# The last layer's value chunk moved from one PSUM bank to another in a four-layer attention and expert kernel

## The chip, the cores and the metric

One core of a Trainium2 chip runs the whole program. The time is device microseconds (us) from one launch, and lower is better. The engines named below are PE (TensorE, matmuls; PEld are its weight loads), DVE (VectorE), ACT (ScalarE), POOL (GpSimd) and SP (SyncE, which issues DMAs). Each engine runs its own list of instructions in the order written; they meet at semaphores only. PE writes into PSUM, which has eight banks of 128 partitions x 512 fp32 values; ACT and DVE read results out of it. A bank may be written again only when the engine that reads it is done, and that is what the waits in this case are about.

## The reference

Input x is 32 batches x 128 rows x 128 columns. Four layers follow each other, each an attention over a fixed context and then a feed-forward part, always as x = x + f(layernorm(x)): layer 0 and layer 3 have a top-2 mixture of 8 experts, layer 1 a quantised gated unit, layer 2 a router over 64 slots with a GRU step. The last layer's attention, which the change touches, is

```
q = x @ Wq                                  # 128 -> 1024 = 16 heads of 64
k, v = split(context @ Wkv)                 # 128 -> 2048
attn = softmax(q k^T / 8) per head
out = concat(attn @ v) @ Wout + bout        # 1024 -> 128
```

## The kernel before

x stays in SBUF. The 32 batches are handled in 8 groups of 4 (512 rows a group). The program has three phases; the third is where layer 1's down projection, layers 2 and 3 and the last experts are interleaved. Its time is cut into half steps `hs`. In each half step every engine has a list of short pieces, called `work(place, hs)`, at three places (0, 1, 2) between the fixed pieces of one attention unit (scores, exps, transposes, values times probabilities). Tables written by hand say which piece goes where.

A unit of layer 2 is 8 heads of one batch. A unit of layer 3 is a chunk of two heads for the 4 batches of a group; 8 chunks make a group. Layer 3's chunks stand at every second half step. For chunk c of group g:

- three half steps ahead, PE forms the query chunk (line 1774, "q" below) at place 0, and the key chunk (line 1781, "k") at place 2 of the same half step;
- two half steps ahead, PE forms the value chunk (lines 1807, "V" below, 8 records since each fp32 matmul shows as two) at place 2, and ACT copies it from PSUM to SBUF (line 2106, semaphore `v_row`);
- the output chunk of every second unit (line 1790) and layer 2's output row (line 1799) stand at place 0 of the half steps that hold a V.

PSUM is dealt out like this: banks 0 and 1 hold scores, `BANK_T` the transposes, `BANK_PV` the products with the values, `BANK_X` and `BANK_Z` the expert tiles. `BANK_A` serves q, k, V, the output chunk and the output row one after the other. `BANK_B` is the side bank: the layernorm transposes (`turn_y`, line 1714), layer 2's projections and the whole chain of the slot router pass through it. `bank_a(reader)` and `bank_b(reader)` make PE wait until the previous user of that bank has been read, and note who will read the new content:

```
def bank_b(reader):
    if read_b:
        pe.wait_ge(*read_b[-1])
    read_b.append(reader)
```

Pieces of the side bank that the prediction names, with the place and the reader of each: line 1843, first product of the slot router, read by ACT's gelu (line 2090, at place 2, ahead of the V copy); line 1857, slot inputs; line 1886, transposes of the new slots; line 1901, second half of the slots' output; line 1714, layernorm transposes, read by ACT (line 2079); lines 421 and 423, ranks of the expert sort, read by DVE (line 449, semaphore `moe_index`). Other lines: 1740 and 1751 are an expert tile's two products, 1977 and 1984 the scores of layers 2 and 3, 2036 the transposes of probabilities, 2193 ACT's copy of the first half of these, 2233 POOL's normalisation of half a unit's probabilities, 2338 DVE's last step on an expert tile, 2493 DVE's last step of the GRU.

The q of the following half step stands right behind V on PE, but for what is put between: the scores of the next unit, where that is one of layer 2 and the expert tiles have begun; an expert tile; a piece of the side bank.

Of the kernel before, what the change touches and what calls it, by code (L numbers as in the profile page):

```python
# [30 lines left out]
ACT = mybir.ActivationFunctionType  # L31
# [4 lines left out]
B, S, D = 32, 128, 128  # L36
# [6 lines left out]
IC3 = H * DH3 // P  # L43
# [67 lines left out]
def build(nc, x_d, ctx_d, ctxT_d, mask0_d, mask1_d, w_d, r_d, rank_d, we0_d, we3_d, big3_d, wg_d, wu_d, wd_d, out_d):  # L111
    with ExitStack() as stack:
# [66 lines left out]
        ps = stack.enter_context(nc.psum_tensor("ps", [P, 8, 512], F32))  # L179

        def W(name, p=P):
            a, n = W_AT[name]
            return w[0:p, a:a + n]
# [368 lines left out]
        for key in sorted(tile_table, key=lambda key: (key[1], key[2])):  # L552
            g, kind, t = tile_table[key]
# [908 lines left out]
        def find(times, hs):  # L1462
            for g, at in enumerate(times):
                if at == hs:
                    return g
            return None

        def pro_at(hs, offset):
            return find([at[0] + offset for at in L2_AT], hs)

        def slot_at(hs, offset):
            return find([at + offset for at in SLOT_AT], hs)

        def moe_at(hs, offset):
            return find([at + offset for at in MOE_AT], hs)

        NDW = E3 - NW3
        BANK_T, BANK_PV, BANK_A, BANK_B, BANK_X, BANK_Z = range(2, 8)
# [57 lines left out]
        def score_bank(n):  # L1536
            return BANK_X if n in alternating and n % 2 else 0
# [9 lines left out]
        for hs, place, item in order:  # L1547
            g, kind, i = item
# [21 lines left out]
        def slot512(n, count=1):  # L1570
            return h_all[:, n:n + count, :].rearrange("p a t -> p (a t)")
# [5 lines left out]
        ctx3 = [mask1i[:, :, :].bitcast(F32).rearrange("p b k -> p (b k)"), xg[:, :, :].rearrange("p b d -> p (b d)")]  # L1577
# [26 lines left out]
        v3 = [slot512(17), slot512(18)]  # L1604
# [18 lines left out]
        n2 = dict(att_b)  # L1623

        with nc.Block() as block:
# [71 lines left out]
            def _(pe):  # L1697
                read_a, read_b = [], []

                def bank_a(reader):  # L1700
                    if read_a:
                        pe.wait_ge(*read_a[-1])
                    read_a.append(reader)
# [55 lines left out]
                def work(place, hs):  # L1759
# [9 lines left out]
                    if chunk and place == 0:  # L1769
                        g, c = chunk  # L1770
# [5 lines left out]
                    if chunk and place == 2:  # L1776
                        g, c = chunk
# [6 lines left out]
                    if chunk and place == 0:  # L1784
                        g, c = chunk
                        pe.wait_ge(n2["o_read"], number[(3, g, c)] + 1)
                        bank_a((n2["chunk_added"], IC3 // 2 * g + c // 2 + 1))
                        for b in range(G):
                            for e in (c - 1, c):
                                m = pe.matmul(ps[:, BANK_A, b * D:(b + 1) * D], oT3[e % 3][:, b * S:(b + 1) * S],  # L1790
                                              o3_w[:, e, :], start=(e == c - 1), stop=(e == c))
                        m.then_inc(n2["out_psum"], 1)
                    for b in range(G):
                        g = find([at[b] for at in ROW_AT], hs)
                        if g is not None and place == 0:
                            pe.wait_ge(n2["o_read"], number[(2, g, 2 * b + 1)] + 1)
                            bank_a((n2["row_added"], G * g + b + 1))
                            for c in range(2):
                                m = pe.matmul(ps[:, BANK_A, 0:D], ous[(2 * b + c) % 4], wo2[:, c, :],
                                              start=(c == 0), stop=(c == 1))  # L1800
                            m.then_inc(n2["row_psum"], 1)
                    chunk = V_AT.get(hs)
                    if chunk and place == 2:
                        g, c = chunk
                        bank_a((n2["v_row"], IC3 * g + c + 1))
                        for b in range(G):
                            m = pe.matmul(ps[:, BANK_A, b * D:(b + 1) * D], ctx3[g % 2][:, b * S:(b + 1) * S],  # L1807
                                          v3_w[:, c, :], start=True, stop=True)
                        m.then_inc(n2["v_psum"], 1)

                    g = pro_at(hs, -4)
# [8 lines left out]
                    g = pro_at(hs, -3)  # L1820
                    if g is not None and place == 2:
                        turn_y(front, g + 1)
                    g = pro_at(hs, -2)
# [4 lines left out]
                    g = pro_at(hs, -1)  # L1828
                    if g and place == 0:
                        bank_b((v_dve, g))  # L1830
                        for b in range(G):
                            m = pe.matmul(ps[:, BANK_B, b * D:(b + 1) * D], ctl[:, b * S:(b + 1) * S], W("wv2"), start=True,
                                          stop=True)
                        m.then_inc(n2["v2_psum"], 1)

                    g = slot_at(hs, 1)
                    if g is not None and place == 2:
                        turn_y(mid, g + 1)
                    g = slot_at(hs, 2)
# [4 lines left out]
                    g = slot_at(hs, 3)  # L1844
                    if g is not None and place == 0:
                        pe.wait_ge(slot["hid"], g + 1)
                        bank_b((slot["logits_read"], g + 1))
                        for b in range(G):
                            m = pe.matmul(ps[:, BANK_B, b * SLOTS:(b + 1) * SLOTS], gT[:, b * S:(b + 1) * S],
                                          W("w2s", HR), start=True, stop=True)  # L1850
                        m.then_inc(slot["logits"], 1)
                    g = slot_at(hs, 4)
                    if g is not None and place == 2:
# [5 lines left out]
                        for q in range(2):  # L1859
                            m = pe.transpose(ps[:, BANK_B, 256 + q * P:256 + (q + 1) * P],  # L1860
                                             alpha[:, 2 * q:2 * q + 2, :].rearrange("p b s -> p (b s)"), ident)
                        m.then_inc(slot["in_psum"], 1)
                    g = slot_at(hs, 5)
                    if g is not None and place == 0:
                        pe.wait_ge(slot["in_ready"], g + 1)
                        bank_b((slot["xn_in"], g + 1))
                        for b in range(G):
                            q, a = divmod(b, 2)
                            pe.matmul(ps[64 * a:64 * a + 64, BANK_B, 256 + q:257 + q], alpha[:, b, :], ones[:, 0:1],
                                      start=True, stop=True)  # L1870
                        for q in range(2):
                            m = pe.matmul(ps[:, BANK_B, q * D:(q + 1) * D], siT[:, q * P:(q + 1) * P],
                                          W("wih")[:, 2 * D:3 * D], start=True, stop=True)
                        m.then_inc(slot["wsum"], 1)
                    if g is not None and place == 2:
                        bank_b((slot["rz_in"], g + 1))
                        for q in range(2):
                            m = pe.matmul(ps[:, BANK_B, 2 * q * D:2 * (q + 1) * D], siT[:, q * P:(q + 1) * P],
                                          W("wih")[:, 0:2 * D], start=True, stop=True)
                        m.then_inc(slot["gates_psum"], 1)  # L1880
                    g = slot_at(hs, 7)
                    if g is not None and place == 0:
                        pe.wait_ge(slot["new"], g + 1)
                        bank_b((slot["newT"], g + 1))
                        for q in range(2):
                            m = pe.transpose(ps[:, BANK_B, q * P:(q + 1) * P], hnew[:, q, :], ident)
                        m.then_inc(slot["newT_psum"], 1)
                    if g is not None and place == 2:
                        pe.wait_ge(slot["newT"], g + 1)
                        bank_b((slot["val"], g + 1))  # L1890
                        for q in range(2):
                            m = pe.matmul(ps[:, BANK_B, q * D:(q + 1) * D], hnT[:, q * P:(q + 1) * P], W("wvs"), start=True,
                                          stop=True)
                        m.then_inc(slot["val_psum"], 1)
                    g = slot_at(hs, 8)
                    if g is not None and place in (0, 2):
                        a = place // 2
                        pe.wait_ge(slot["val"], g + 1)
                        bank_b((slot["oT"], 2 * g + a + 1))
                        for q in range(2):  # L1900
                            m = pe.matmul(ps[:, BANK_B, q * S:(q + 1) * S], sval[64 * a:64 * a + 64, q, :],
                                          aT[64 * a:64 * a + 64, q, :], start=True, stop=True)
                        m.then_inc(slot["oT_psum"], 1)
                    g = slot_at(hs, 9)
                    if g is not None and place == 0:
                        pe.wait_ge(slot["oT"], 2 * g + 2)
                        bank_b((slot["out_read"], g + 1))
                        for b in range(G):
                            m = pe.matmul(ps[:, BANK_B, b * D:(b + 1) * D], outT[:, b * S:(b + 1) * S], W("wos"),
                                          start=True, stop=True)  # L1910
                        m.then_inc(slot["out_psum"], 1)
                    g = slot_at(hs, 10)
# [3 lines left out]
                    g = moe_at(hs, 1)  # L1916
                    if g is not None and place == 2:
                        turn_y(experts, g + 1)
                    g = moe_at(hs, 2)
# [4 lines left out]
                    g = moe_at(hs, 4)  # L1924
# [3 lines left out]
                    g = pro_at(hs, -2)  # L1928
# [93 lines left out]
                for hs in range(FIRST, LAST + 1):  # L2022
# [5 lines left out]
                    for half in range(2):  # L2028
                        if p is not None:
# [5 lines left out]
                            for k in range(4):  # L2035
                                m = pe.transpose(ps[:, BANK_T, k * S:(k + 1) * S],  # L2036
                                                 pb[:, p % 2, (4 * half + k) * S:(4 * half + k + 1) * S], ident)
# [12 lines left out]
            def _(a):  # L2050
# [30 lines left out]
                def work(place, hs):  # L2081
# [3 lines left out]
                    g = slot_at(hs, 2)  # L2085
# [6 lines left out]
                    if chunk and place == 1:  # L2092
                        g, c = chunk
# [6 lines left out]
                    if chunk and place == 2:  # L2100
                        g, c = chunk
                        a.wait_ge(n2["v_psum"], IC3 * g + c + 1)
                        before = number[(3, g, c - 2)] if c >= 2 else number[(3, g - 1, c + IC3 - 2)] if g else None
                        if before is not None:
                            a.wait_ge(n2["pv"], before + 1)
                        a.activation(v3[c % 2], ps[:, BANK_A, :], ACT.Copy).then_inc(n2["v_row"], 1)  # L2106

                    g = pro_at(hs, -3)
                    if g is not None and place == 2:
# [3 lines left out]
                    g = pro_at(hs, -2)  # L2113
# [11 lines left out]
                    g = slot_at(hs, 1)  # L2125
# [4 lines left out]
                    g = slot_at(hs, 3)  # L2130
# [3 lines left out]
                    g = slot_at(hs, 4)  # L2134
# [3 lines left out]
                    g = slot_at(hs, 5)  # L2138
# [3 lines left out]
                    g = slot_at(hs, 6)  # L2142
# [3 lines left out]
                    g = slot_at(hs, 7)  # L2146
# [3 lines left out]
                    g = slot_at(hs, 8)  # L2150
# [6 lines left out]
                    g = slot_at(hs, 10)  # L2157
# [5 lines left out]
                    g = moe_at(hs, 1)  # L2163
# [4 lines left out]
                    g = moe_at(hs, 2)  # L2168
# [6 lines left out]
                for hs in range(FIRST, LAST + 1):  # L2175
                    n, p = unit_at.get(hs), unit_at.get(hs - 1)
                    for half in range(2):
                        if n is not None:
# [4 lines left out]
                            for k in range(4):  # L2183
                                e = 4 * half + k
                                m = a.activation(pb[:, n % 2, e * S:(e + 1) * S], ps[:, score_bank(n) + half, k * S:(k + 1) * S], ACT.Exp,  # L2185
                                                 bias=nm[:, n % 2, e:e + 1], accum_out=sums[:, 8 * (n % 2) + e:8 * (n % 2) + e + 1])
# [9 lines left out]
                    if p is not None:  # L2196
                        _, layer, g, t = units[p]
# [6 lines left out]
                        else:  # L2204
# [3 lines left out]
                            elif t >= 3:  # L2208
                                a.wait_ge(n2["out_psum"], IC3 // 2 * g + (t - 3) // 2 + 1)
                            a.activation(oT3[t % 3], ps[:, BANK_PV, :], ACT.Copy).then_inc(n2["o_read"], 1)  # L2210
                    work(2, hs)
                    if hs == DENSE_AT:
                        for i in range(2 * E3 + 2):
# [473 lines left out]
```

## Time and profile before

| | us |
|---|---|
| median of 3 runs | 2080.22 |
| lowest, highest run | 2069.82, 2084.04 |
| profiled execution, its own time | 2070.54 |
| its span | 2068.8 |
| PE busy, share of the span | 1836.7, 89% |
| DVE, ACT, POOL busy | 1477.0, 1282.5, 637.5 |

The span runs from the first to the last instruction, so 1.7 us lie around it. PE is the busiest engine. The third phase's chunks of layer 3 lie between about 1010 us and 1960 us of the span. A row with a bracket says how long the engine stood idle before that instruction and which instruction on another engine ended the wait; a row without one means that the engine came straight from its own instruction before. Records of the same line that follow each other are merged, with their count behind an x and their total time in front.

### The profile page before, as it was taken

To read this page: it belongs to the slowest core of one execution; us is meant where nothing else is said; L and a number is where in the kernel's file an instruction comes from. 1 tells how busy PE (TensorE), PEld (TensorE's weight loads), DVE (VectorE), ACT (ScalarE), POOL (GpSimd) and SP (SyncE) were. 2 spreads that over 40 slices of the span, in tenths; PEclk is the share of its full clock that TensorE was granted. 3 is DMA by queue.
4 is the path that set the end of the run, shared out by engine and by line. 5 is a ranking of instruction groups with operands and counts; after the bars stand their busy time and mean duration, and the time that the engine had idled before them with its cause. 6 is when DMAs were issued, how large, how long until landed. Compare 5 with 4: busy or idle time off the path is not lost.

```text
span 2068.8 us, 49634 instructions
## 1 busy us (share of the span) xinstructions
PE 1836.7 (89%) x17477; PEld 1495.0 (72%) x17477; DVE 1477.0 (71%) x3859; ACT 1282.5 (62%) x4466; POOL 637.5 (31%) x653
## 2 busy tenths in 40 slices
PE   7898999989999996677888889999999998888879
PEld 6777888878788775565666667777777776767665
DVE  7987978878788885767675766767667574655546
ACT  6876666656667785456677766666676654555422
POOL 2212122423222301133433353353543424232311
PEclk9999999999999997877899999999999999999999
DMA  8013454544543102200000022222312222232341
GB/s 264 17 63 107 134 177 141 171 122 132 159 150 109 31 7 79 90 20 26 26 1 21 1 66 66 81 66 87 96 56 86 73 85 80 88 93 85 120 135 38
DMA packets 129733, 178.30 MB, mean 86 GB/s; under 512 B 10192, under 2 KB 91024, under 8 KB 129232
## 3 DMA queue, kind: packets, MB, share of 16 engines
q1 hardware_dynamic: 121808, 159.38, 25.3%
q0 software_dynamic: 7680, 15.74, 2.4%
q8 instruction: 143, 2.34, 0.4%
q14 instruction: 102, 0.84, 0.1%
HBM read 141.13 MB, written 33.95 MB: 85 GB/s over the span
## 4 chain that ended last, share of the span: by engine, by line
PE 37%; DVE 9%; ACT 6%; issue 5%; POOL 1%; DMA 0%; DVEq 0%; ACTq 0%; SPq 0%
PE ps L1740 5%; PE ps L2036 5%; PE ps L1790 3%; PE ps L1984 3%; PE ps L1977 3%; ACT pb L2185 3%; PE ps L1774 3%; PE ps L1781 2%; PE ps L1958 2%; PE ps L1751 2%; DVE nm L2569 2%; PE ps L2006 1%; PE ps L1807 1%; PE ps L1951 1%; DVE hT L2333 1%
## 5 line engine op out<-in xcount | busy, mean ns | idle before, releaser
L2185 ACT ACTIVATE pb<-ps,nm 128x128 f32<-128x128 f32 x1024 | 363.4, 377 | 194.7 <-DVE nm L2569 193.0
L2233 POOL TENSOR_TENSOR pb<-pb,rcs 128x512 f32<-128x512 f32 x256 | 268.7, 1050 | 653.1 <-DVE rcs L2577 652.2
L978 ACT ACTIVATE pb<-pb,nm 128x128 f32<-128x128 f32 x1024 | 312.9, 393 | 37.4 <-DVE nm L1290 35.5
L2594 DVE COPY pt<-ps 128x512 f32<-128x512 f32 x128 | 88.3, 690 | 194.0 <-PE ps L2036 193.6
L2185 ACT ACTIVATION_READ_ACCUMULATOR pb<-ps,nm 128x1 f32 x1024 | 222.2, 217 | 0.0
L2569 DVE TENSOR_REDUCE nm<-ps 128x8 f32<-128x1024 f32 x128 | 155.9, 1218 | 61.8 <-PE ps L1984 39.2
L2036 PE MATMUL ps<-w,pb 128*128 128x128 f32 x1024 | 167.4, 288 | 25.1 <-ACT pt L2193 12.5
L1290 DVE TENSOR_REDUCE nm<-pb 128x8 f32<-128x1024 f32 x128 | 156.2, 1220 | 4.4
L2036 PEld LDWEIGHTS ps<-w,pb 128*128 128x128 f32 x1024 | 120.9, 147 | 49.5 <-ACT pt L2193 22.6
L858 PE MATMUL ps<-w,pb 128*128 128x128 f32 x1024 | 141.3, 279 | 9.8 <-ACT pb L978 9.5
L2193 ACT ACTIVATE pt<-ps 128x512 f32<-128x512 f32 x128 | 77.0, 601 | 91.5 <-PE ps L2036 91.4
L1740 PE MATMUL ps<-hT,big 128*128 128x128 f32 x840 | 117.1, 283 | 15.3 <-DVE hT L2338 13.5
L858 PEld LDWEIGHTS ps<-w,pb 128*128 128x128 f32 x1024 | 118.7, 144 | 16.2 <-issue 11.8
L1740 PEld LDWEIGHTS ps<-hT,big 128*128 128x128 f32 x840 | 105.1, 195 | 34.9 <-DVE hT L2338 22.9
L970 ACT ACTIVATE pt<-ps 128x512 f32<-128x512 f32 x128 | 76.3, 596 | 66.9 <-PE ps L858 66.0
L712 PE MATMUL ps<-h_all,big 128*128 128x128 f32 x736 | 104.3, 286 | 12.6 <-DMA big<-in_we 5.1
L712 PEld LDWEIGHTS ps<-h_all,big 128*128 128x128 f32 x736 | 93.4, 198 | 20.0 <-ACT hT L903 6.2
L720 PE MATMUL ps<-big,hT 128*128 128x128 f32 x736 | 101.6, 282 | 0.0
L2067 ACT ACTIVATE hT<-ps 128x256 f32<-128x256 f32 x133 | 51.0, 383 | 75.2 <-PE ps L1740 74.6
L720 PEld LDWEIGHTS ps<-big,hT 128*128 128x128 f32 x736 | 92.8, 197 | 5.6 <-issue 2.4
L1774 PE MATMUL ps<-h_all,big 128*128 128x512 f32 x128 | 72.4, 648 | 26.4 <-ACT h_all L2106 26.4
L1751 PE MATMUL ps<-big,hT 128*128 128x128 f32 x532 | 89.9, 292 | 2.1 <-DVE hT L2338 2.1
(383 smaller groups left out, 4326.8 us busy)
## 6 DMA issues: line engine op xcount, KB each, us to landing
big<-in_we SPq DMA_DIRECT2D x92, 514.0 KB, 3.8
big<-in_we SPq DMA_DIRECT2D x109, 384.0 KB, 3.1
sorted_out<-big SPq DMA_DIRECT2D x27, 256.0 KB
big<-sorted_in SPq DMA_DIRECT2D x7, 960.0 KB, 6.4
sorted_in<-big SPq DMA_DIRECT2D x4, 1472.0 KB, 12.5
big<-sorted_in SPq DMA_DIRECT2D x20, 256.0 KB, 3.9
hidden<-h_all SPq DMA_DIRECT2D x7, 512.0 KB, 2.9
h_all<-hidden SPq DMA_DIRECT2D x7, 512.0 KB, 3.8
```

The source lines that it names most:

```text
L712: m = pe.matmul(ps[:, 5, c * P:(c + 1) * P], w1_0[:, k % NWS, c, :], xsT0[:, (NQ0 * g + t // 4) % 4, (t % 4) * P:(t % 4 + 1) * P], start=T ...
L720: m = pe.matmul(ps[:, 7, (t % 4) * D:(t % 4 + 1) * D], hT[:, k % 4, c * P:(c + 1) * P], w2_0[:, k % NWS, c, :], start=(c == 0), stop=(c == ...
L858: m = pe.transpose(ps[:, 2 + k // 4, (k % 4) * S:(k % 4 + 1) * S], pb[:, p % 2, k * S:(k + 1) * S], ident)
L978: m = a.activation(pb[:, n % 2, k * S:(k + 1) * S], pb[:, n % 2, k * S:(k + 1) * S], ACT.Exp, bias=nm[:, n % 2, k:k + 1])
L1290: v.tensor_reduce(nm[:, n % 2, :], buf, AX, ALU.max, negate=True).then_inc(s["maxed"], 1)
L1740: m = pe.matmul(ps[:, bank, (2 * half + c) * P:(2 * half + c + 1) * P], weights[:, half, c, :], rows_T, start=True, stop=True)
L1751: m = pe.matmul(ps[:, z_bank[(g, q)], at:at + D], hid[k % 4][:, c * P:(c + 1) * P], weights[:, 2, c, :], start=(c == 0), stop=(c == C3 - 1))
L1774: pe.matmul(ps[:, BANK_A, :], q3_w[:, c, :], yT3[g % 2], start=True, stop=True)\
L2036: m = pe.transpose(ps[:, BANK_T, k * S:(k + 1) * S], pb[:, p % 2, (4 * half + k) * S:(4 * half + k + 1) * S], ident)
L2185: m = a.activation(pb[:, n % 2, e * S:(e + 1) * S], ps[:, score_bank(n) + half, k * S:(k + 1) * S], ACT.Exp, bias=nm[:, n % 2, e:e + 1], a ...
L2233: g_.tensor_tensor(p4, p4, r4.unsqueeze(2).to_broadcast([P, 4, S]), ALU.mult).then_inc(n2["p_normed"], 1)
L2569: v.tensor_reduce(nm[:, n % 2, :], ps[:, bank:bank + 2, :].rearrange("p a (j k) -> p (a j) k", k=S), AX, ALU.max, negate=True).then_inc(n2 ...
```

## The change

The value chunk's matmuls write `BANK_B` in place of `BANK_A`, guarded by `bank_b`, and ACT's copy reads `BANK_B`. Nothing is added, removed or put in another order on any engine.

```
@@ work(place, hs) of PE @@
                         g, c = chunk
-                        bank_a((n2["v_row"], IC3 * g + c + 1))
+                        bank_b((n2["v_row"], IC3 * g + c + 1))
                         for b in range(G):
-                            m = pe.matmul(ps[:, BANK_A, b * D:(b + 1) * D], ctx3[g % 2][:, b * S:(b + 1) * S],
+                            m = pe.matmul(ps[:, BANK_B, b * D:(b + 1) * D], ctx3[g % 2][:, b * S:(b + 1) * S],
                                           v3_w[:, c, :], start=True, stop=True)
                         m.then_inc(n2["v_psum"], 1)
@@ work(place, hs) of ACT @@
-                        a.activation(v3[c % 2], ps[:, BANK_A, :], ACT.Copy).then_inc(n2["v_row"], 1)
+                        a.activation(v3[c % 2], ps[:, BANK_B, :], ACT.Copy).then_inc(n2["v_row"], 1)
```

What changes is which semaphore each user of the two banks waits for. Three places on PE show it; a semaphore's name in brackets is what the instruction waits for (the last letters tell apart attention semaphores), and the rows with - are the kernel before.

PE, the V of a half step that also holds the transposes of the layernorm ahead of layer 2's attention (`y_ready_front`; `down_read` is DVE's read of the down projection, the side bank's user before):

```order
-L1807 MATMUL ps<-big,xg 128x128 [waits row_added_b]
+L1807 MATMUL ps<-big,xg 128x128 [waits down_read_b]
 L1807 MATMUL ps<-big,xg 128x128 x3
-L1714 MATMUL ps<-w,y 128x128 [waits down_read_b,y_ready_front]
+L1714 MATMUL ps<-w,y 128x128 [waits v_row_b,y_ready_front]
 L1714 MATMUL ps<-w,y 128x128 x3
 L1751 MATMUL ps<-big,hT 128x128 [waits moe_hid_dve]
```

The transposes directly behind V now wait for ACT's copy of V, and V for a reader of the side bank.

PE, the V of the half step in which the slot router's first product stands at place 0 (`slot_hid` is the gelu that reads it; `chunk_added` DVE's read of the output chunk), in the part with expert tiles:

```order
-L1807 MATMUL ps<-big,mask1i 128x128 [waits chunk_added_b]
+L1807 MATMUL ps<-big,mask1i 128x128 [waits slot_hid]
 L1807 MATMUL ps<-big,mask1i 128x128 x3
 L1740 MATMUL ps<-hT,big 128x128 [waits weights_loaded_2,moe_xT,moe_hid_dve]
 L1740 MATMUL ps<-hT,big 128x128 x3
-L1774 MATMUL ps<-h_all,big 128x512 [waits v_row_b]
-L1849 MATMUL ps<-w,h_all 128x64 [waits slot_hid]
+L1774 MATMUL ps<-h_all,big 128x512 [waits chunk_added_b]
+L1849 MATMUL ps<-w,h_all 128x64 [waits v_row_b,slot_hid]
 L1849 MATMUL ps<-w,h_all 128x64 x3
```

V now waits for the gelu; q no longer waits for ACT's copy of V, and the next product of the slot router does.

PE, a V whose half step and the next hold no piece of the side bank, in the last stretch:

```order
-L1807 MATMUL ps<-big,xg 128x128 [waits chunk_added_b]
+L1807 MATMUL ps<-big,xg 128x128 [waits v_row_b]
 L1807 MATMUL ps<-big,xg 128x128 x3
-L1774 MATMUL ps<-h_all,big 128x512 [waits v_row_b]
+L1774 MATMUL ps<-h_all,big 128x512 [waits chunk_added_b]
 L1740 MATMUL ps<-hT,big 128x128 [waits weights_loaded_0,moe_xT,moe_hid_dve]
 L1740 MATMUL ps<-hT,big 128x128 x3
```

V waits for the copy of the V before it, and q for DVE's read of the output chunk.

## Rows read from the trace of the kernel before

**Rows 1.** The page: busy time of each engine, share, instructions

```profile
PE 1836.7 (89%) x17477; PEld 1495.0 (72%) x17477; DVE 1477.0 (71%) x3859; ACT 1282.5 (62%) x4466; POOL 637.5 (31%) x653
```

**Rows 2.** Windows: length; busy of PE, PEld, DVE, ACT, POOL; clock; DMA share, GB/s

```profile
1015.00:1230.00 215.00, 188.39 (x1791) 141.17 (x1791) 145.85 (x395) 150.14 (x623) 88.86 (x84) 0.98 0.07 23
1230.00:1635.00 405.00, 392.21 (x3652) 316.78 (x3649) 277.30 (x802) 273.38 (x1091) 167.76 (x162) 1.00 0.25 75
1635.00:1960.00 325.00, 287.36 (x2330) 229.44 (x2330) 183.07 (x522) 163.12 (x579) 106.42 (x104) 0.99 0.29 87
```

**Rows 3.** Waits of PE, 1015 to 1230: releaser, us in total, times, longest

```profile
PE ps L1774 <- ACT h_all L2106: 7.6, 12, 0.8
PE ps L2036 <- ACT pt L2193: 2.8, 5, 1.1
```

**Rows 4.** Waits of PE, 1230 to 1635: the largest

```profile
PE ps L1740 <- DVE hT L2338: 4.7, 9, 0.7
```

**Rows 5.** Waits of PE, 1635 to 1962

```profile
PE ps L1774 <- ACT h_all L2106: 18.8, 20, 1.9
...
PE ps L2036 <- POOL pb L2233: 2.5, 4, 0.8
```

**Rows 6.** Timeline, third stretch: start us, length us, engine, line, what

```profile
1751.91 1.05 PE L1807 MATMUL ps<-big,mask1i 128*128 128x128 f32 x8
1753.01 0.60 ACT L2106 ACTIVATE h_all<-ps 128x512 f32<-128x512 f32 x1 [0.29 <-PE ps L1807]
...
1753.66 1.13 PE L1774 MATMUL ps<-h_all,big 128*128 128x512 f32 x2 [0.69 <-ACT h_all L2106]
```

**Rows 7.** Timeline, second stretch: V, front transposes, copy of V

```profile
1363.00 1.06 PE L1807 MATMUL ps<-big,mask1i 128*128 128x128 f32 x8
1363.89 0.60 PE L1714 MATMUL ps<-w,y 128*128 128x128 f32 x4
...
1364.88 0.63 ACT L2106 ACTIVATE h_all<-ps 128x512 f32<-128x512 f32 x1
```

**Rows 8.** Timeline, second stretch: two slot pieces behind V, with V's copy

```profile
1300.15 1.00 PE L1857 MATMUL ps<-h_all 128*128 128x64 f32 x8
1300.35 0.60 ACT L2106 ACTIVATE h_all<-ps 128x512 f32<-128x512 f32 x1 [0.24 <-PE ps L1807]
...
1333.57 0.71 PE L1901 MATMUL ps<-h_all,ou 64*128 64x128 f32 x4
1333.95 0.67 ACT L2106 ACTIVATE h_all<-ps 128x512 f32<-128x512 f32 x1
```

**Rows 9.** Timeline, second stretch: V and the gelu of its half step

```profile
1411.07 1.06 PE L1807 MATMUL ps<-big,xg 128*128 128x128 f32 x8
...
1412.81 1.16 PE L1740 MATMUL ps<-hT,big 128*128 128x128 f32 x8 [0.68 <-DVE hT L2338]
1413.23 0.68 ACT L2090 ACTIVATE h_all<-ps,c 64x512 f32<-64x512 f32 x1
...
1413.89 1.16 PE L1977 MATMUL ps<-kT,qm 32*128 32x128 f32 x16
```

**Rows 10.** Timeline, first stretch: V and the gelu of its half step

```profile
1154.65 1.06 PE L1807 MATMUL ps<-big,xg 128*128 128x128 f32 x8
1155.33 0.68 ACT L2090 ACTIVATE h_all<-ps,c 64x512 f32<-64x512 f32 x1
```

**Rows 11.** Timeline, second stretch: V, the ranks' reader, next slot piece

```profile
1447.18 1.06 PE L1807 MATMUL ps<-big,xg 128*128 128x128 f32 x8
...
1447.69 0.16 DVE L449 CAST big<-cmp_a 128x4 int32<-128x4 f32 x1
...
1451.20 0.44 PE L1886 MATMUL ps<-w,h_all 128*128 128x128 f32 x2 [0.82 <-DVE h_all L2493]
```

**Rows 12.** Windows around two of PE's long waits, columns as in rows 2

```profile
1185.00:1192.00 7.00, 4.40 (x32) 2.93 (x34) 6.55 (x23) 2.89 (x12) 1.16 (x2) 0.92 0.01 2
...
1222.00:1232.00 10.00, 7.11 (x66) 5.73 (x66) 7.87 (x25) 4.72 (x22) 3.46 (x4) 1.00 0.37 101
```

## The prediction

> **What bounds the kernel now.** I read the page first: PE is busy for 89% of the span, DVE for 71, ACT for 62 [rows 1]. A microsecond in which PE stands still is therefore usually lost, and one on the others usually is not. Then the windows, because the change lies in the third phase only. They give three stretches [rows 2]. In the first (layer 2 and layer 3 units, two score banks, 15 V) PE is busy 188.4 of 215 us. In the second (the expert tiles have joined, 25 V) it is busy 392.2 of 405: 97%, the most in the program. In the third (layer 2's units are over, 24 V) 287.4 of 325. Then PE's waits in each stretch, for one reason: the wait that the change takes away is that of q (line 1774) for ACT's copy of V (line 2106). It is 7.6 us in 12 places of the first stretch [rows 3] and 18.8 us in 20 places of the third [rows 5]. In the second it is not in the list at all, and nothing in that list is larger than 4.7 us [rows 4]: there the next unit's scores, about 1 us, stand between V and q and cover the copy. So at most 7.6 + 18.8 = 26.4 us can be had, 1.3% of the span, and none of it where PE is fullest.
>
> A plain place shows how it comes about [rows 6]. V starts at 1751.91, ACT copies it from 1753.01 to 1753.61, and q starts at 1753.66, 0.05 after the copy, having waited 0.69.
>
> **What the change puts in its place.** No instruction is added, so the whole cost is in waits, and PE runs its list in order: whatever waits holds up everything behind it, scores, transposes and tiles. The side bank is no idle bank. In every group that has a slot chain, four of eight V have a piece of the side bank directly behind them, and two more have one ahead whose reader is late. I price each kind at a row.
>
> - Slot inputs (line 1857) behind V: they start at 1300.15; with the copy ending at 1300.95 and 0.05 behind it they would start at 1301.00: 0.85.
> - Second half of the slots' output (line 1901) behind V: copy ends 1334.62, so 1334.67 in place of 1333.57: 1.10 [rows 8].
> - Late layernorm transposes (line 1714, `y_ready_late`) behind V: the same pattern as line 1857, ACT idle and waiting for V; 0.85.
> - Front transposes (line 1714, `y_ready_front`) behind V: here ACT is still at its exps when V is done, the copy ends at 1365.51, so 1365.56 in place of 1363.89: 1.67 [rows 7].
> - V behind the slot router's first product: ACT's gelu ends at 13.23 + 0.68 = 1413.91, and V, which started at 1411.07, starts at about 1413.96. The tile behind it had waited 0.68 for DVE until 1412.81, which is now over before it is reached. V takes 1.00 until the next matmul, the tile 1.08, so the scores start at 1416.04 in place of 1413.89: 2.15 net of 2.9 [rows 9]. In the first stretch the gelu ends at 1156.01 and V had started at 1154.65: 1.4 [rows 10].
> - V behind the ranks: DVE's last step ends at 1447.85, V had started at 1447.18, so 0.7 late; but the next slot piece (line 1886) waits 0.82 for the GRU step anyway [rows 11], which does not depend on this V. Nothing lost, except that a q wait saved there is not gained either.
> - V behind the value projection of layer 2, the router logits or the first half of the slots' output: in the second stretch their readers end before V starts. Nothing. V behind a V, plain: nothing.
>
> What hides a stall is a later wait of PE on something that is not itself late. If such waits were everywhere, each of these prices would be 0; if nowhere, each is what stands above. I take the full price in the second stretch, where a 97% busy PE leaves little to hide in, and look for cover in the other two.
>
> **The sum, by stretch.**
>
> Second stretch, 0 removed. Three line 1857 at 0.85 = 2.6; three line 1901 at 1.10 = 3.3; three late transposes at 0.85 = 2.6; three front transposes at 1.67 = 5.0; three gelu at 2.15 = 6.5. Together +19.9.
>
> First stretch, 7.6 removed. Six places have a side bank piece directly behind V, at 0.85 to 1.1: 5.9. PE's waits for ACT's copy of the first transposes come after five of the 15 V, 2.8 us in all, up to 1.1 each [rows 3]. ACT reaches that copy by its exps and not by q, so such a wait hides one of the six (0.85), and two q waits (1.2) are given back in it. The gelu costs 1.4. The ranks take away one q gain (0.8). -7.6 + 1.2 + 5.9 - 0.85 + 1.4 + 0.8 = +0.9.
>
> Third stretch, 18.8 removed. Four times the transposes wait for POOL's normalisation, 2.5 us in all [rows 5]: two of them give back a q gain of 0.8 each, and the two others hide the stall of late transposes (0.6 of 0.85 each). The longest q gain, 1.9, I count at half, an estimate: the same POOL step would be next to end late. Two groups still have their slot chain. Each costs 0.85 (line 1857), 1.8 (line 1901: q waits of up to 1.9 show that ACT's copy comes that late here, where it is at its exps), 0.25 (late transposes), 2.9 (gelu, with no wait of the tile to set against it), 0.7 (ranks), 6.5 together. -18.8 + 2.6 + 2 x 6.5 = -3.2.
>
> All in all +0.9 + 19.9 - 3.2 = **+17.6 us**, slower by 0.8%. Both ends of the unknown, which is how much is hidden: all gains and no stall -26.4; all stalls and no gain 8.1 + 19.9 + 13.0 = +41. The value taken lies nearer to the stalls, because the stretch with no gain is the one in which PE stands still least [rows 2].
>
> Against the profiled execution's own 2070.54 (span 2068.8 and 1.7 around it) this is 2088.1. The median of the three runs is 9.7 above that execution, and would give 2097.8. One run is at the profiled level and two are 10 to 14 above, so I put the forecast at the middle of the two scales: **2093**.
>
> **Weighed against a rule.** The row of the plain place shows PE standing 0.69 us because two groups of matmuls follow each other in one bank [rows 6]. The Trainium skill, page "Perfetto Trace Analysis", section "Matmuls", says that independent groups of matmuls should rotate through different PSUM banks, so that one group's evacuation overlaps the next group's matmuls; by that alone the sum would be -26.4. The trace agrees where V is followed by q, and differs where V is followed by a piece of the bank it moves to [rows 7, 8]: there the rotation was there before, and the change takes it away.
>
> **The rivals.**
>
> *The rotation wins: faster.* The side bank's new stalls fall into waits that PE has later anyway, and q's 26.4 us are gained. For it: q's waits are the largest of their stretches [rows 3, 5], and the tiles' waits for DVE [rows 4] can hide stalls. Against it: those are 4.7 us in 9 places, for stalls of 19.9 in 15. With all stalls hidden 2044 on the profiled scale, 2054 at the median; from 18 of the 41 us of stalls hidden on it is faster than before at all, and from 38 on by over 1%. Chance of the latter 0.04.
>
> *They cancel: no change.* Gains as summed, but half of the second stretch's stalls are hidden, by tiles' waits on DVE and by units in which ACT or DVE and not PE closes the loop. -3.2 + 0.9 + 10 = +8, between -5 and +9: 2066 to 2080, or 2075 to 2089 at the median. Chance 0.23.
>
> *The stalls breed: clearly slower.* A later V makes ACT's copy late, behind which the next unit's exps are queued; and PE's clock falls in the holes. Where PE was busy for 4.40 of 7 us the granted clock was 0.92 of full speed, so part of that time at 1.2 in place of 2.4 GHz, and in a stretch with 7.11 of 10 it stayed at 1.00 [rows 12]. The gelu's holes of 2.9 us are longer than any of the waits that they replace (up to 1.9 [rows 5]); there are five of that size. At 1 us lost for each, and up to all gains not made, +25 to +46: 2096 to 2117 (2105 to 2126). Chance 0.18.
>
> *The change does not do what it says.* The order on every engine is the same and only the waits differ, so q is free of the copy; no chance is put on this.
>
> **The numbers.** The forecast's own range, +9 to +25, has 0.55 and lies at 2080 to 2096, or 2089 to 2105 at the median. About 1%, 20.7 us, is what a measurement of this kernel can tell from no change: slower by more than that are the worst rival (0.18) and the upper part of the forecast's range (0.16), 0.34; faster 0.04; within it 0.62. The range leaves out the top of the breeding stalls and most of the gain: **2073 to 2112**.
>
> **What would show it.** In the changed kernel's trace: q's waits on line 2106 gone; waits on line 2106 at lines 1714, 1857 and 1901 instead, 0.8 to 1.9 each; V (line 1807) waiting about 2.9 for line 2090 in the second and third stretch; PE's busy share of the second stretch down from 97% to about 92, the second stretch's V-to-V distance longer by some 6.6 us a group and the third's unchanged or shorter. If PE's idle time in the second stretch grows by less than 10 us, the stalls were hidden and the price of the second stretch was wrong. If it grows by more than 25, the copies themselves came later than today's rows say.

## The result, and the profile after

The changed kernel takes 2115.82 us (median; 2108.77 to 2123.36) against 2078.76 before (2069.82 to 2084.04): 1.0173 times as long, 95% interval 1.0133 to 1.0213. That is 37 us more, where 17.6 were forecast, and just outside the forecast's range. The profiled execution took 2108.77 us with a span of 2107.0, 38.2 more than the span before.

The page of the changed kernel, busy time of each engine, against [rows 1]:

```profile
PE 1860.8 (88%) x17473; PEld 1510.1 (72%) x17477; DVE 1475.9 (70%) x3859; ACT 1286.4 (61%) x4466; POOL 638.4 (30%) x653
```

PE's share fell by one point, but its busy time grew by 24.1 us with the same instructions (4 of the matmul records are missing from the trace after). Waits add idle time; they cannot add busy time. So something made the matmuls themselves longer. The three stretches in the changed kernel, with their bounds moved so that the same V lie in each, against [rows 2]:

```profile
1015.00:1232.00 217.00, 189.41 (x1790) 141.07 (x1790) 146.09 (x397) 151.00 (x623) 89.09 (x84) 0.98 0.07 23
1232.00:1678.00 446.00, 415.56 (x3658) 332.21 (x3655) 277.63 (x803) 276.13 (x1093) 168.00 (x162) 0.95 0.22 68
1678.00:2001.00 323.00, 288.53 (x2334) 230.07 (x2333) 183.00 (x522) 164.78 (x581) 106.60 (x104) 0.98 0.29 88
```

The whole loss is in the second stretch. PE's idle time there is 446.0 - 415.6 = 30.4 us, and was 405 - 392.2 = 12.8: 17.6 more. Its busy time is 23 us more, and the granted clock is 0.95 in place of 1.00. The first and the third stretch are as long as before, within 2 us.

PE's waits in the second stretch of the changed kernel (columns as in [rows 3]):

```profile
PE ps L1807 <- ACT h_all L2090: 8.2, 3, 2.7
PE ps L1714 <- ACT h_all L2106: 7.2, 6, 1.6
PE ps L1901 <- ACT h_all L2106: 3.0, 3, 1.1
PE ps L1740 <- DVE hT L2338: 2.7, 6, 0.7
PE ps L1857 <- ACT h_all L2106: 2.3, 3, 0.8
PE ps L1807 <- DVE big L449: 1.7, 3, 0.6
```

These are the new waits the prediction named, in their places and sizes: gelu 2.7 (priced 2.9 before the tile's wait is set off), front transposes 1.6 (1.67), slots' output 1.1 (1.10), slot inputs 0.8 (0.85), ranks 0.6 (0.7). The only row here that was there before is the tiles' wait for line 2338, 4.7 in 9 places in [rows 4].

The plain place of [rows 6], V 48 in the changed kernel's timeline:

```profile
1796.88 1.06 PE L1807 MATMUL ps<-big,mask1i 128*128 128x128 f32 x8
1797.77 1.02 PE L1774 MATMUL ps<-h_all,big 128*128 128x512 f32 x2
1797.97 0.60 ACT L2106 ACTIVATE h_all<-ps 128x512 f32<-128x512 f32 x1 [0.29 <-PE ps L1807]
```

q now starts without a wait and ahead of ACT's copy, as forecast. V and the front transposes, V 23, against [rows 7]:

```profile
1375.33 1.06 PE L1807 MATMUL ps<-big,mask1i 128*128 128x128 f32 x8
1377.22 0.63 ACT L2106 ACTIVATE h_all<-ps 128x512 f32<-128x512 f32 x1
1378.00 0.63 PE L1714 MATMUL ps<-w,y 128*128 128x128 f32 x4 [1.61 <-ACT h_all L2106]
```

The transposes stood 0.89 behind the start of V, and now 2.67. And the gelu's half step, V 26, against [rows 9]:

```profile
1429.02 0.68 ACT L2090 ACTIVATE h_all<-ps,c 64x512 f32<-64x512 f32 x1
...
1429.76 1.16 PE L1807 MATMUL ps<-big,xg 128*128 128x128 f32 x8 [2.74 <-ACT h_all L2090]
1430.75 1.83 PE L1740 MATMUL ps<-hT,big 128*128 128x128 f32 x8
...
1432.51 2.08 PE L1977 MATMUL ps<-kT,qm 32*128 32x128 f32 x16
1434.52 2.08 PE L1774 MATMUL ps<-h_all,big 128*128 128x512 f32 x2
```

Here the missing time shows. Behind the hole of 2.74 us the scores (line 1977) take 2.08 us, where they took 1.16 in [rows 9], and q 2.08, where it took 1.13 in [rows 6]: 1.8 times as long, close to half speed. The windows of the changed kernel around this place say for how long (columns as in [rows 2]; the granted clock is the third figure from the end, 1.00 in the first line):

```profile
1410.00:1430.00 20.00, 16.96 (x151) 13.05 (x150) 13.72 (x40) 14.82 (x55) 10.45 (x10) 1.00 0.34 105
1430.00:1434.00 4.00, 4.00 (x30) 3.78 (x31) 0.84 (x4) 1.96 (x3) 1.04 (x1) 0.60 0.42 161
1434.00:1440.00 6.00, 6.00 (x32) 3.78 (x34) 3.36 (x9) 2.24 (x10) 0.00 (x0) 0.50 0.00 0
1440.00:1446.00 6.00, 5.89 (x36) 4.55 (x29) 2.87 (x9) 2.61 (x12) 1.04 (x1) 0.63 0.22 66
1446.00:1453.00 7.00, 6.56 (x69) 5.78 (x69) 6.72 (x26) 4.27 (x18) 1.04 (x1) 1.00 0.36 96
```

The window with the hole is still at full clock. The fall comes behind it, and TensorE then runs at the lower of its two levels, 1.2 GHz, for most of the next 16 us, although it is busy all the time. That fits a sentence of the Trainium skill, page "Perfetto Trace Analysis", section "Matmul Optimizations": "The matmul engine dynamically scales power based on utilization, so it's important that matmuls execute back-to-back in batches."

To see it place by place I took from each trace the start of every V (k is 8 times the group plus the chunk), and compared the distances. The third phase begins between 1024 and 1039 us in the profiled executions shown below, before anything of the change, so only distances inside it are compared. A step below is the distance from one V to the next, named by the first of the two ("behind V 26" is from V 26 to V 27):

```
us from V 0 to 14 / 14 to 39 / 39 to 63    (first, second, third stretch)
before            189.4   407.2   336.3
changed           190.6   447.7   333.7
difference         +1.2   +40.5    -2.6     (forecast +0.9, +19.9, -3.2)
```

Windows bounded by the same V split each difference. PE's idle time changed by +1.2, +17.4 and -3.2 us, its busy time by 0.0, +23.1 and +0.6. The forecast of +0.9, +19.9 and -3.2 comes within 2.5 us of the idle time in each stretch; what it lacks is the busy time of the second.

### The profile page after: what moved, and what is told of

It is laid out like the page before. It is cut to its first block, busy times and chain, and to the rows that moved or that the text cites. A ratio compares the mean times of both kernels' runs of the same rounds, so it can differ in the third digit from the quotient of the medians.

```text
span 2107.0 us, 49630 instructions
## 1 busy us (share of the span) xinstructions
PE 1860.8 (88%) x17473; PEld 1510.1 (72%) x17477; DVE 1475.9 (70%) x3859; ACT 1286.4 (61%) x4466; POOL 638.4 (30%) x653
## 4 chain that ended last, share of the span: by engine, by line
PE 36%; DVE 10%; ACT 7%; issue 5%; POOL 2%; DMA 0%; DVEq 0%; ACTq 0%; SPq 0%
PE ps L1740 5%; PE ps L2036 4%; ACT pb L2185 3%; PE ps L1977 3%; PE ps L1790 3%; PE ps L1984 2%; PE ps L1774 2%; DVE nm L2569 2%; PE ps L1751 2%; PE ps L1958 2%; PE ps L1781 2%; PE ps L1807 1%; PE ps L2006 1%; PE ps L1951 1%; DVE hT L2333 1%
## 5 line engine op out<-in xcount | busy, mean ns | idle before, releaser
L1740 PE MATMUL ps<-hT,big 128*128 128x128 f32 x840 | 122.4, 292 | 15.1 <-DVE hT L2338 11.9
L1740 PEld LDWEIGHTS ps<-hT,big 128*128 128x128 f32 x840 | 109.8, 203 | 35.8 <-DVE hT L2338 23.2
L712 PEld LDWEIGHTS ps<-h_all,big 128*128 128x128 f32 x736 | 92.5, 196 | 20.7 <-issue 6.4
L963 ACT ACTIVATE ou<-ps 128x128 f32<-128x128 f32 x128 | 34.9, 273 | 85.7 <-DVE h_all L1272 47.6
```

The costliest lines, as they stand in the source:

```text
L712: m = pe.matmul(ps[:, 5, c * P:(c + 1) * P], w1_0[:, k % NWS, c, :], xsT0[:, (NQ0 * g + t // 4) % 4, (t % 4) * P:(t % 4 + 1) * P], start=T ...
L1740: m = pe.matmul(ps[:, bank, (2 * half + c) * P:(2 * half + c + 1) * P], weights[:, half, c, :], rows_T, start=True, stop=True)
```

## The experiments

The theory after this was A: about half of the 40 us of the second stretch are the stalls as priced, and half is TensorE's clock, which falls behind them. The rivals were B, that the holes are simply longer than priced and the slow matmuls a by-product that costs nothing of its own; and C, that the side bank itself is slower for V, for instance because its readers and PE's writes get in each other's way. Each run below is compared with the kernel before on the same chip, by ratio of times with its 95% interval.

**The holes filled with work** (throwaway matmuls of the identity into bank A, whose reader is waited for first):

```
+                    def fill(count):
+                        pe.wait_ge(*read_a[-1])
+                        for k in range(count):
+                            pe.matmul(ps[:, BANK_A, k % 4 * P:(k % 4 + 1) * P], ident, ident, start=True, stop=True)
...
+                        if FILL_BEFORE.get(hs):      # 9 where the gelu stands
+                            fill(FILL_BEFORE[hs])
                         bank_b((n2["v_row"], IC3 * g + c + 1))
...
+                        if FILL_BEHIND.get(hs):      # 2, 3, 2, 5 where a side bank piece stands behind V
+                            fill(FILL_BEHIND[hs])
```

> The changed kernel with throwaway matmuls into bank A in PE's new holes (from slot group 3 on: 9 ahead of the V that waits for the gelu; behind V 2 ahead of the slot inputs, 3 ahead of the slots' output, 2 ahead of the late, 5 ahead of the front transposes); nothing else changes. Theory A (half of the loss is TensorE's clock, which falls in the holes): the granted clock of the second stretch goes back from 0.95 to about 1.00, the stretch shrinks from 446 us by 15 to 22, total about 18 below the changed kernel, 2085 to 2095 beside a before of 2070 to 2080 (+0.8%). Theory B (the holes are simply longer than priced, the clock is a by-product): total as the changed kernel, +1.7%.

Measured 1.0074 (1.0050 to 1.0097), median 2095.58. More work in the program, and it takes 20 us less than the changed kernel. Its second stretch:

```profile
1251.00:1677.00 426.00, 409.03 (x3781) 331.61 (x3780) 275.75 (x795) 275.30 (x1091) 169.05 (x164) 1.00 0.24 71
```

The clock is back at 1.00, and the stretch is 426 us where it was 446. Nor does this hang on one trace: the mean clock of whole executions is 0.954 to 0.964 in the ten of this run, and 0.944 to 0.955 in the changed kernel's four. Theory A holds, B falls: V stays as late (the step up to each V behind a gelu is 2.9 us longer than in the kernel before, here and in the changed kernel), but the stalls are no longer empty. V 14 to 39 takes 429.4, 18.3 less than the changed kernel. Step by step the changed kernel is longer at seven places: behind V 18, 19, 23, 29 and 31 by 1.6 to 1.7 us each, and behind V 26 and 34 by 5.9 and 5.8. Those seven come to 19.8. (At an eighth, behind V 14, this run is 1.5 longer; its clock falls there.) Taken from the changed kernel's 40.5 they leave 20.7 for the stalls, priced at 19.9.

**The gelu's half steps alone, and the front transposes' alone** (V in the side bank there, else in bank A):

```
+        def value_bank(g, c):
+            hs, k = L3_AT[g][c] - 2, IC3 * g + c
+            return BANK_B if hs in [at + 2 for at in SLOT_AT[2:]] else BANK_A     # first run
+            return BANK_B if hs in [at[0] - 3 for at in L2_AT] else BANK_A        # second run
...
-                        bank_b((n2["v_row"], IC3 * g + c + 1))
+                        v_bank = value_bank(g, c)
+                        (bank_b if v_bank == BANK_B else bank_a)((n2["v_row"], IC3 * g + c + 1))
```

> V in the side bank only in the 6 half steps in which the slot router's gelu stands (V 10, 18, 26, 34, 42, 50), else in bank A as before. Stalls alone: 3 x 2.15 + 2 x 1.35 + 0.6 = +10 us. Theory A (clock falls behind each hole of 2.9 us): another 4 to 5 us for each of five holes, +25 to +32, the granted clock of the second stretch near 0.97. Theory B: +10, clock 1.00.

Measured 1.0076 (1.0053 to 1.0099), median 2093.3: +14 to +16, between the two. The steps of the profiled execution tell why; it is the fastest of the run's ten, with the highest mean clock (0.960, the others 0.949 to 0.958), so others may hold more falls. Each of the three holes in the second stretch costs 2.05 net by itself (priced 2.15). Behind V 34 another 6.0 are lost, behind V 18 another 1.4, and behind V 26, after the same hole, nothing. Windows of this run around V 26 (the hole ends at 1415.7) and V 34 (1548.2):

```profile
1396.00:1416.00 20.00, 16.97 (x151) 13.07 (x150) 13.76 (x40) 14.75 (x55) 10.44 (x10) 1.00 0.35 106
1416.00:1420.00 4.00, 4.00 (x36) 3.00 (x34) 1.90 (x5) 2.27 (x3) 1.04 (x1) 1.00 0.41 153
1420.00:1426.00 6.00, 5.48 (x51) 4.26 (x52) 5.13 (x18) 4.34 (x20) 1.04 (x1) 1.00 0.21 65
...
1528.00:1548.00 20.00, 17.15 (x153) 13.26 (x152) 13.70 (x43) 14.74 (x55) 10.43 (x10) 0.99 0.33 96
1548.00:1552.00 4.00, 3.81 (x18) 3.59 (x18) 1.25 (x6) 0.73 (x2) 1.04 (x1) 0.50 0.04 15
1552.00:1558.00 6.00, 6.00 (x27) 4.16 (x28) 2.06 (x4) 3.17 (x10) 0.00 (x0) 0.50 0.01 3
1558.00:1564.00 6.00, 5.47 (x38) 3.94 (x38) 3.91 (x14) 2.47 (x10) 1.04 (x1) 0.73 0.18 48
```

PE does the same work ahead of both holes (16.97 and 17.15 busy of 20 us), and once the clock falls, at the very end of the hole and behind it, and once it does not. A hole makes a fall possible, not certain; what decides was not tried.

> V in the side bank only in the half steps with the front transposes (V 7, 15, 23, 31). Stalls alone: 3 x 1.67 + 0.5 = +5.5 us. Theory A: V to V distance of 3.4 in place of 1.7 us longer behind V 23 and 31, as in the changed kernel, so +9, with the granted clock below 1.00 there. Theory B: +5.5, clock 1.00.

Measured 1.0044 (1.0023 to 1.0066), median 2087.52, +9. The steps from V 15, 23 and 31 grew by 1.80, 1.79 and 3.43: the stall near its price (1.67) three times, and 1.6 of clock once, not twice (the granted clock is 0.50 from 1511.5 to 1514.5, behind V 31 at 1506.96). In the changed kernel both of the latter two had it. No V of this run waits for a gelu, so a hole of 1.6 us can be followed by a fall by itself.

**Only the gelu's holes filled** (the first run's code with the 9 ahead of V alone; its expectation names a jump of 1.6 by the V at its end, so V 20, 24, 30 and 32 there are the steps behind V 19, 23, 29 and 31 here):

> The changed kernel with throwaway matmuls only ahead of the V that waits for the gelu (9, from slot group 3 on); the holes of 0.8 to 1.7 us behind V stay empty. If the clock falls behind the long holes alone: as the run with all holes filled, +0.75%. If the short holes let it fall too (four jumps of 1.6 us in the changed kernel stand behind V 20, 24, 30, 32, where no gelu is): between, +1.0 to +1.3%, with jumps of 1.6 left there and those of 5 behind V 26 and 34 gone. Theory B (no clock): +1.7%.

Measured 1.0084 (1.0052 to 1.0115), median 2095.61, which the interval does not tell from all holes filled. V 14 to 39 takes 429.5. The jumps of 5.8 are gone, and of the five jumps of 1.6 one is left, behind V 23. So my reading that the short holes let the clock fall by themselves holds here for that one at most, and for one in the run with the front transposes alone; three of the four jumps that I had put down to them are missing where the long holes alone were filled. Why is not shown, with one execution profiled of each.

**The waits without the bank** (the kernel before, V in bank A, with the side bank's waits added):

```
+                        if read_b:
+                            pe.wait_ge(*read_b[-1])
+                        read_b.append((n2["v_row"], IC3 * g + c + 1))
                         bank_a((n2["v_row"], IC3 * g + c + 1))
```

> The kernel before, V in bank A as there, but with the changed kernel's waits of the side bank added: V waits for the side bank's last reader, and the next user of the side bank for V's copy. Nothing moves to another bank. If waits (and the clock behind them) are the whole loss: second stretch +40 us as in the changed kernel, and the gains of the plain places (some 13 us) are missing as well, +50 in all, +2.4%. Rival C (the side bank is slower for V, or ACT's and DVE's reads of it collide with PE's writes): clearly less than the changed kernel's +40 in the second stretch.

Measured 1.0285 (1.0249 to 1.0322), median 2138.49. Its second stretch and the waits in it (line numbers are 3 higher than in the changed kernel):

```profile
1257.00:1701.00 444.00, 413.10 (x3662) 329.87 (x3661) 275.72 (x795) 276.19 (x1093) 169.27 (x164) 0.96 0.22 68
```

```profile
PE ps L1810 <- ACT h_all L2093: 8.2, 3, 2.7
PE ps L1714 <- ACT h_all L2109: 7.2, 6, 1.6
PE ps L1904 <- ACT h_all L2109: 3.0, 3, 1.1
```

V 14 to 39 grows by 39.5, as in the changed kernel, with V still in bank A, and the waits are the same to a tenth. Rival C falls: the waits, with the clock behind them, are the whole loss to within 1 us, and the bank has no part in it that can be seen. In all this run lost 60, not 50: its first stretch grew by 14.4. The added waits and q's old ones are both paid there, but that is the smaller part: PE's idle time grew by 3.7 and its busy time by 10.7, at a granted clock of 0.92 where the kernel before had 0.98.

**The fillers where there are no holes** (the kernel before, with the first run's matmuls, all ahead of V):

> The kernel before with the fillers of the first run (9 + 2 + 3 + 2 + 5 throwaway matmuls a group from slot group 3 on), all ahead of V, where it has no holes: what the fillers cost by themselves. About 0.24 us each where PE has no hole, 21 x 0.24 = 5 us for each of three groups in the second stretch and some less in the third, +10 to +20 us, +0.5 to +1.0%, clock unchanged. If fillers by themselves made the program faster (a clock held up elsewhere), 0 or below.

Measured 1.0046 (1.0023 to 1.0069), median 2090.56; V 14 to 39 takes 420.1, 12.9 more than before, of which 1.6 is a fall of the clock behind V 14. Its second stretch, from V 15 on:

```profile
1247.00:1663.00 416.00, 405.16 (x3775) 330.05 (x3775) 275.36 (x795) 274.93 (x1090) 168.91 (x163) 1.00 0.24 73
```

Fillers cost their time where PE is full. They paid in the first run only because they stood in holes.

**The side bank where nothing of it is near** (and, in the second run, at eight more such places where q had not waited):

```
+            return BANK_B if k in (4, 5, 6, 8, 9, 40, 41, 47, 48, 49) or k >= 55 else BANK_A
+            # second run: also 1, 16, 17, 24, 25, 32, 33, 39
```

> V in the side bank only where neither a piece of it stands behind V nor a late reader ahead, and where q waited for V's copy: V 4, 5, 6, 8, 9, 40, 41, 47, 48, 49 and 55 to 63; else in bank A. If q's waits were really lost time: -0.7 -0.6 -0.7 -0.7 -0.2 in the first stretch and -9.2 in the third, -12 us, 0.994 of before. Rival: the gained time is spent in PE's next waits (for DVE, POOL, ACT), 0 to -4.

Measured 0.9911 (0.9889 to 0.9934), median 2061.22: faster than before and than the changed kernel. Its three stretches:

```profile
1020.00:1237.00 217.00, 192.87 (x1825) 144.93 (x1825) 149.52 (x405) 152.98 (x633) 89.17 (x85) 0.97 0.07 23
1237.00:1643.00 406.00, 393.14 (x3661) 317.46 (x3659) 276.01 (x796) 274.62 (x1095) 169.68 (x165) 1.00 0.25 75
1643.00:1952.00 309.00, 279.36 (x2288) 222.95 (x2288) 181.59 (x518) 159.53 (x561) 103.66 (x102) 0.99 0.31 92
```

V 0 to 14 takes 186.1 (-3.2), 14 to 39 407.2 (0.1 more), 39 to 63 324.4 (-11.9): 15.1 gained where 12 were worked out. 1.6 of it lies between V 50 and 51, where nothing of the edit is: the clock falls twice there in the trace of the kernel before (0.50 from 1784.8 to 1788.2 and 0.51 from 1795.0 to 1798.4), and once in this one. The waits of q that are left in the third stretch, against 18.8 in 20 places in [rows 5] (q is line 1778 in this run, and ACT's copy 2111):

```profile
PE ps L1778 <- ACT h_all L2111: 6.9, 8, 1.4
```

> As the run with V in the side bank at clean places, and also at eight more where no side bank piece collides but q does not wait either (V 1, 16, 17, 24, 25, 32, 33, 39). Waits theory: the same as that run, 0.991 of before, second stretch unchanged against before. Rival C (the side bank itself is slower): slower than that run, and V to V distances in the second stretch longer behind these V.

Measured 0.9917 (0.9887 to 0.9947), median 2060.76, and the steps in the second stretch are those of the kernel before to 0.03 us. V in the side bank costs nothing where no neighbour waits for it.

## Why the prediction was wrong

- **What bounds the kernel.** Right: the second stretch, where PE is fullest and q had nothing to give, decides.
- **The removed waits.** Right. q waits for V's copy nowhere in the changed kernel, and by the clean places run the gain is real time.
- **The new waits.** Right in place and size: idle time +17.4 in the second stretch between the same V, and 20.7 for the stalls by the steps, for 19.9.
- **What hides a stall.** Right. Full price in the second stretch, cover in the others: idle time +1.2 and -3.2 measured, +0.9 and -3.2 forecast. The sign that the prediction named for itself, idle time of the second stretch up by 10 to 25, came out too, and the time was still wrong: that sign cannot see longer matmuls.
- **The clock.** This is the step that failed: "At 1 us lost for each, and up to all gains not made" in the rival of the breeding stalls, and no term at all for it in the sum. The clock took 19.8 us in the second stretch, more than the forecast's whole sum: 5.9 and 5.8 behind two of its three gelu holes, 1.6 behind the third, and 1.6 to 1.7 at four places with no gelu, which the rival did not count. I priced it from a window that holds a wait ([rows 12], 0.92 and 1.00). Nearly all of the low clock lies behind the hole and not in it: the window of the changed kernel that holds the gelu's hole shows 1.00 too, and the next 16 us show 0.50 to 0.63. The 0.92 of [rows 12] was the beginning of such a fall. The wait there ends at 1190.64; the windows of the kernel before up to that point and behind it, which [rows 12] does not have, show it:

```profile
1186.00:1190.90 4.90, 2.30 (x13) 1.28 (x12) 4.62 (x16) 1.65 (x6) 1.04 (x1) 1.00 0.00 0
1191.00:1194.00 3.00, 3.00 (x31) 2.21 (x31) 2.54 (x7) 2.24 (x10) 1.31 (x2) 0.50 0.03 5
```

- **The rivals.** The worst one, given 0.18, came true in size (+25 to +46) and in one of its two mechanisms. Its other one, that ACT's copy and the next unit's exps become late, did not: with the holes filled the stretch costs what the stalls cost. The rotation did not win, and the cancelling did not happen.
- **Expectations behind the result.** The filled holes, the clean places and the fillers' own cost came out as theory A said, and so did the second stretch of the waits without the bank, though that run lost 10 more elsewhere. Three came out otherwise: the gelu run lies between its two values, the front transposes had one fall and not two, and filling the gelu's holes alone took away three of the four jumps that were put down to shorter holes.

## What to carry to other kernels

A bank that two in-order chains share couples their waits: before work moves into it, list for each half step which user stands directly ahead and behind, and who reads it when. Moving only the uses without neighbours took 0.9% off; moving all of them added 1.7%. And where TensorE is nearly full, a hole can have a second price behind it in clock. Here holes of 0.8 to 2.7 us cost 20.7 themselves in the second stretch, and 19.8 more by the clock. Read the granted clock in the windows after a wait, not only in the one that holds it.

## What the runs showed that was not expected

- Behind a hole of 2.74 us the granted clock was 0.60, 0.50 and 0.63 over the following 4, 6 and 6 us, with PE busy for 15.9 of these 16. Such an event cost 5.8 to 6.0 us; the smaller ones cost 1.4 to 1.7.
- The same hole, after the same work, was followed by a fall in one execution or place and not in another (V 26 in the changed kernel and in the gelu run). With it goes the spread of the runs: of the changed kernel's four, two took about 2109 us at mean clocks of 0.951 and 0.955, and two 2122 and 2123 at 0.944.
- Throwaway matmuls in the holes made the changed kernel faster by 20 us; the same matmuls where there were no holes made the kernel before slower by 10 to 12.
